# Summing q's squares with the squares as the stationary operand, one column of ones moving

## The reference, cut to what matters

```python
def _rmsnorm(x, w):
    var = jnp.mean(xf * xf, axis=-1, keepdims=True)      # over the 128 numbers of a head
    return (xf * jax.lax.rsqrt(var + EPS)).astype(x.dtype) * w
q = _rmsnorm(q, q_norm_w)
scores = jnp.einsum('bhqd,bhkd->bhqk', q, k) * scale
probs = jax.nn.softmax(scores.astype(jnp.float32), axis=-1)
```

## Time and profile before

| | us |
|---|---|
| median of three runs | 1466.25 |
| lowest, highest | 1464.45, 1468.65 |
| the profiled execution | 1465.77 |
| its span, first to last instruction | 1464.0 |
| TensorE busy | 1419.2 (97% of the span) |
| VectorE busy | 847.3 (58%) |
| ScalarE busy | 501.0 (34%) |
| GpSimd busy | 317.9 (22%) |

### The profile page before, as it was taken

How to read it: one execution, slowest core, us unless ns; L and a number is a source line. 1 busy time by engine, 2 the same in 40 slices (tenths; PEclk the granted TensorE clock), 3 DMA queues, 4 the chain that set the end, 5 groups by cost and what they waited for, 6 DMA issues and landing times.

```text
span 1464.0 us, 27092 instructions
## 1 busy us (share of the span) xinstructions
PE 1419.2 (97%) x9085; PEld 1128.1 (77%) x9086; DVE 847.3 (58%) x1816; ACT 501.0 (34%) x1097; POOL 317.9 (22%) x330
## 2 busy tenths in 40 slices
PE   6999997999999999999999999999999999999995
PEld 5888876787777877778787777877777888777773
DVE  5444446565666656666565666656687653344375
ACT  4333343333333333333333333333334421222220
POOL 1222223212122121211212121121212101232462
PEclk9999999999999999999999999999999999999997
DMA  6544440111111111111101111111122343655565
GB/s 225 164 122 136 122 118 30 47 30 40 37 40 40 30 47 37 34 36 40 41 29 49 37 33 39 38 40 33 59 71 81 126 170 138 230 164 170 153 195 171
DMA packets 91097, 125.95 MB, mean 86 GB/s; under 512 B 7376, under 2 KB 56528, under 8 KB 90512
## 3 DMA queue, kind: packets, MB, share of 16 engines
q1 hardware_dynamic: 84704, 104.16, 22.5%
q0 software_dynamic: 6320, 20.71, 5.1%
HBM read 87.36 MB, written 37.49 MB: 85 GB/s over the span
## 4 chain that ended last, share of the span: by engine, by line
PE 91%; issue 3%; DVE 2%; DMA 2%; POOL 1%; ACT 1%; SPq 0%; POOLq 0%; DVEq 0%; ACTq 0%
PE ps L549 23%; PE ps L551 22%; PE ps L550 22%; PE ps L879 5%; PE ps L615 4%; PE ps L657 4%; PE ps L895 3%; PE ps L623 2%; PE ps L642 2%; PE ps L874 1%; PE ps L596 1%; DMA acc<-in_wv 1%; DMA wgu<-in_w_gu 1%; DVE acc L1660 1%; PE ps L793 1%
## 5 line engine op out<-in xcount | busy, mean ns | idle before, releaser
L1046 ACT CAST ah<-ps 128x256 fp32r<-128x256 f32 x256 | 83.4, 382 | 238.5 <-PE ps L551 234.6
L470 POOL CAST vth<-vt 128x256 fp32r<-128x256 f32 x64 | 25.7, 402 | 637.6 <-PE ps L657 637.6
L1284 DVE TENSOR_TENSOR acc<-ps,acc 128x512 f32 (+1 forms) x129 | 88.6, 687 | 129.9 <-PE ps L551 129.9
L549 PE MATMUL ps<-hT,w0h 128*128 128x512 f32 (+1 forms) x384 | 153.9, 401 | 0.9 <-DVE w0l L1232 0.9
L551 PE MATMUL ps<-hT,w0h 128*128 128x512 f32 (+1 forms) x384 | 150.6, 392 | 0.0
L550 PE MATMUL ps<-hT,w0l 128*128 128x512 f32 (+1 forms) x384 | 150.0, 391 | 0.0
L464 POOL TENSOR_TENSOR qr<-qv,mhalf 128x8 f32<-128x8 f32 x64 | 105.6, 1649 | 90.0 <-DVE qv L1299 90.0
L1290 DVE TENSOR_TENSOR al<-ps,ah 128x256 fp32r<-128x256 f32 x256 | 95.7, 416 | 50.6 <-ACT ah L1046 50.6
L1013 ACT COPY qs<-ps 128x512 f32<-128x512 f32 x128 | 75.2, 587 | 134.9 <-PE ps L551 131.4
L1022 ACT ACTIVATE pb<-pb 128x256 f32<-128x256 f32 x128 | 48.2, 418 | 175.3 <-DVE pb L1315 175.3
L549 PE MATMUL ps<-w1l,ah 128*128 128x512 f32 x260 | 105.3, 405 | 1.0 <-DVE al L1290 1.0
(11 more groups left out here) (223 smaller groups left out, 3033.8 us busy)
## 6 DMA issues: line engine op xcount, KB each, us to landing
wraw<-in_w_att SPq DMA_DIRECT2D x64, 256.0 KB, 2.6
ybuf<-ye SPq DMA_DIRECT2D x47, 256.0 KB, 2.0
vbuf<-vo SPq DMA_DIRECT2D x16, 512.0 KB, 3.3
kbuf<-ko SPq DMA_DIRECT2D x16, 512.0 KB, 3.8
kt<-kbuf SPq DMA_DIRECT2D x32, 256.0 KB, 2.9
vt<-vbuf SPq DMA_DIRECT2D x64, 128.0 KB, 2.0
wgu<-in_w_gu SPq DMA_DIRECT2D x4, 2048.0 KB, 9.3
craw<-in_ctxT SPq DMA_DIRECT2D x9, 512.0 KB, 4.9
```

The source lines that it names most:

```text
L549: pe.matmul(dst, l_hi, r_lo, start=first, stop=False)
L1046: act.copy(ah[:, bp, :, b2, :], pv_view(bp, b2)).then_inc(a_hi, 1)
L1284: dve.tensor_tensor(dst, PS[6 + bp][:], dst, ALU.add).then_inc(acc_done, 1)
```

## The change

`q_sums` has its operands swapped. The squares of one head and one sequence, `sq[:, h, b]` (128 rows, 64 columns), are the weights, and one column of ones moves. A matmul gives 64 sums, one in each of 64 rows, in column `b` of bank 2; head 0 goes to rows 0 to 63 and head 1 to rows 64 to 127. Sixteen matmuls of one column stand in place of four of 256 columns. The sums then lie as the scores do, and VectorE reads the eight columns of bank 2 straight into `qv`. Its transpose, the tile `sst` and the semaphore `ss_turned` go; TensorE's two waits for `ss_turned` are for `q_var` now.

```diff
             def q_sums(j):
                 pe.wait_ge(q_sq, 2 * j + 2)
-                for r in range(4):
-                    s0 = 32 * (r % 2)
-                    mm = pe.matmul(PS[2][32 * r:32 * r + 32, 0:256], ones32[:], sq[:, r // 2, :, s0:s0 + 32],
-                                   start=True, stop=True)
+                for b in range(2 * CB):
+                    for h in range(2):
+                        mm = pe.matmul(PS[2][h * S:(h + 1) * S, b:b + 1], sq[:, h, b], ones32[:, 0:1],
+                                       start=True, stop=True)
                 mm.then_inc(ss_done, 1)
...
                 if last:
-                    pe.wait_ge(ss_turned, i + 1)
+                    pe.wait_ge(q_var, i + 1)
                     transpose_h2(0, 2)
...
                 if first:
                     pe.wait_ge(s_scaled, 1)
-                    pe.wait_ge(ss_turned, 1)
+                    pe.wait_ge(q_var, 1)
...
                 dve.wait_ge(ss_done, j + 2)
-
-                dve.transpose(sst[:].rearrange("p b r -> p (b r)"), PS[2][:, 0:256]).then_inc(ss_turned, 1)
-                dve.wait_ge(ss_turned, j + 1)
-                dve.tensor_scalar(qv[:], sst[:, :, 0], HD * EPS, None, ALU.add).then_inc(q_var, 1)
+                dve.tensor_scalar(qv[:], PS[2][:, 0:8], HD * EPS, None, ALU.add).then_inc(q_var, 1)
```

More of the change, by code:

```diff
@@ L152, in build @@
             pb = sb("pb", [P, 8, S], F32, a)
-            sst = sb("sst", [P, 8, 32], F32, a)
             pt = [sb(f"pt{'hl'[q]}", [P, 4, HG * S], F32R, a) for q in range(2)]
@@ L238, in build @@
             sem("s_sum"), sem("s_rcp"), sem("p_ready"))
-        ss_turned, v_split, pT_hi = sem("ss_turned"), sem("v_split"), sem("pT_hi")
+        v_split, pT_hi = sem("v_split"), sem("pT_hi")
         pT_done, pT_evac, pv_done, a_hi, a_lo, o_done, acc_done = (
```

## The result

| | before | after |
|---|---|---|
| median of 4 runs, us | 1467.21 | 1489.9 |
| lowest, highest | 1464.45, 1468.65 | 1488.27, 1491.15 |
| profiled execution | 1465.77 | 1490.86 |
| its span | 1464.0 | 1489.1 |

The account below looks back on a forecast made before the run. TensorE was taken to bound the kernel, with VectorE's time free from the third step on. 62 steps growing 0.32 us, less 0.3 at the start, add 19.5 us to 1465.77: 1485 us, range 1475 to 1496.

Parts of the forecast that it names:

- The bound: Whole kernel: TensorE, busy 97%, sets the time; removing VectorE's transpose, 0.47 us a step, is worth nothing in 62 steps.
- The terms at the two ends: First two steps: 0.3 us shorter in all; the last steps were counted among the 62 that grow.
- The pace of a pair, 0.058 us: Sums on TensorE: loading 64 fp32 weight columns holds each pair of passes at 0.058 us, as in the scores.
- The rival by which the pace goes with what moves: Sums: with one moving column a pair takes 25 ns, each step wins 0.21 us, kernel 1452 us; chance 0.06.
- passes in line: Sums: 32 passes of 25 ns one after another, growth 0.19 us a step, kernel 1477 us; chance 0.08.
- the prediction's upper bound: Sums: 16 pairs at 0.065 us, L841's pace, plus the whole 0.15 us switch; growth 0.48 us a step.
- The term of a step: Scores' last pass to the output projection: 1.03 us instead of 0.71, so each step grows by 0.32 us.
- the switch to the projection: Between the sums' last pass and the output projection's full array: 0.10 us.
- the forecast of 1.03 us for the new block: Scores' last pass to the projection: 0.93 us to the sums' last pass plus 0.10 for the switch.
- a forecast of 19.5 for steps and ends: Whole kernel: 62 steps growing by 0.32 us, 19.8 us, less 0.3 at the start.
- No change (a gap takes it up): Projection's first load, which stood 0.41 us with nothing named, would absorb up to that growth; kernel 1466 us; chance 0.04.
- The clock: Each step: longer low streaming drops the granted clock, six projection matmuls lose 1.3 us more, kernel 1566 us; chance 0.03.

Follow-up runs that it names:

- experiment 8: Kernel before with VectorE's transpose done twice in each softmax, one after the other; 1469.23 us, ratio 1.0022, middle steps still 14.18 us.
- experiment 4: Changed kernel with 32 columns of ones moving in each sums matmul instead of one; step 14.48 us, kernel 1493.45 us.
- experiment 5: Changed kernel with both heads' squares adjacent, 8 fp32 sums matmuls with 128 columns of weights instead of 16 with 64; step 15.37 us, kernel 1557.82 us.
- 6: Changed kernel with sums in 32 matmuls of 32 weight columns, in four quarters of the array; step 14.23 us, kernel 1466.77 us in one run.
- experiment 9: Swapped sums with 128 columns of weights, 8 matmuls, squares and ones in bf16 instead of fp32; 1437.76 us, ratio 0.9797 to the kernel before.
- The kernel without gaps: Changed kernel with 64 unused semaphore increments ahead of TensorE's program, moving its code by 4 KB; 1481.91 us, ratio 1.0102 to the kernel before.
- Experiment 3: Changed kernel with 240 unused semaphore increments ahead of TensorE's first instruction, outer loop's target at place 190 instead of 206; 1510.59 us, increments themselves 38.7 us.
- experiment 2: Kernel before with 80 unused semaphore increments ahead of TensorE's first instruction, outer loop's target at place 206 as in the changed kernel; 1473.87 us, ratio 1.0045.

## Why the prediction was right

**The bound.** That VectorE's transpose is worth nothing in the middle holds: 28.7 us less of VectorE, and the steps are longer (also experiment 8, with the sign turned). The terms at the two ends were off. The prediction let the first two steps become 0.3 us shorter in all; they became 0.33 longer (10.04 and 16.02 us against 10.25 and 15.48). TensorE's two waits in them are 1.9 us shorter together (2.31 and 3.20 against 2.85 and 4.53), but the granted clock from 229 to 250 us is 0.84 instead of 0.92, so TensorE's own work in that stretch takes longer. In the last steps 0.8 us came back: two of the three waits of the earlier trace rows stand there (0.70 at 1094.39 and 1.43 at 1111.56), and the first of them is gone. The prediction had counted those steps among the 62 in which nothing is won.

**The pace of a pair, 0.058 us, and its reason.** From the scores' second pair on it is 0.058, and in the sums it is the same. Experiments 4 to 6 show that the weights' columns set it, for ordinary fp32 matmuls. The rival by which the pace goes with what moves falls with experiment 4; that each pass or instruction has a price of its own (passes in line, 1477) falls with 5 and 6, where half as many instructions take twice as long and twice as many half as long. The rule of the Trainium skill that a matmul of one column takes as long as one of 60 ("TensorEngine Tiling (Array Packing)", Instruction Overhead) fits that 32 columns cost no more than one, but its 25 ns does not give this kernel's time; only the bf16 passes of experiment 9 start every 25 ns. What does is the load's rule ("TensorE: Matmul & The Clock Gate", LDWEIGHTS), columns divided by 1.2: 53 ns for 64, 27 for 32, 107 for 128, each 4 to 5 ns under the pace measured.

One row was misread. L841, the prediction's upper bound and its argument against the rival of what moves, is a transpose: 48 columns move, but its weights have 128 (48*128 in the earlier trace rows), in one pass each. It is not of the scores' form, so it neither bounded the pair nor spoke against that rival. And at 65 ns for 128 fp32 columns it is faster than the 112 ns of experiment 5, so what was found for matmuls does not hold for transposes.

**The term of a step.** 0.32 was said and 0.287 measured, 2.0 us too much over 62 steps. From the scores' last pass to the projection the growth is 0.31 by the starts in the trace. Two parts of it were off, in opposite ways: the sums' second pair follows the first after 0.03 us instead of 0.058, and the switch to the projection was priced at 0.10 and is 0.127. So the forecast of 1.03 us for the new block was met to 0.002 by errors that cancel. Then the projection's first twelve matmuls take 0.025 us less than before, and no run shows why.

**What was missing.** The profiled execution before, the steps' growth and what came back at both ends give 1465.8 + 18.1 - 0.25 - 0.8 = 1482.8. The kernel without gaps took 1481.9 and the kernel after 1489.9. By the steps' lengths 6.6 of the 22.7 us come from the two jumps and from one stretch of half clock behind them, which no term of the prediction has. So that 1485 was near is partly luck: a missing 6.6 us and a forecast of 19.5 for steps and ends, where 17.0 was measured, point opposite ways.

The cause was in the code: 48 more instructions in each of 7 copies of the sums ahead of the outer loop move its target by 336 places. The Trainium skill has the rule ("Runtime: NRT & Kernel Launch", Instruction fetch mechanics): instructions come in blocks of 16 KB, ahead of time only in sequence, and a jump to code outside the window has to wait for its block. The trace agrees: packets of 16 KB, and a wait of 3.3 to 3.4 us at both jumps, in the kernel before as well as after. TensorE itself need not stand still for it. The first wait is covered by what its queue holds; the second, for the block behind the target's, is covered if enough instructions of the target's own block are left, and in the kernel after only three were. By experiment 3 each matmul more in that block takes 0.17 to 0.20 us off the gap.

**No change (a gap takes it up)** fell: the whole growth stands between the scores and the projection (1.64 to 1.97 us). The 0.41 us was idle time of the loads alone, and the sums' own loads fill it now. **The clock** did not fall in the middle steps of the kernel after, except behind the second gap; it did so at the start, as said, and in ten steps of experiment 5.

## What to carry to other kernels

An fp32 matmul with few moving columns costs what its weights' load costs, so before operands are swapped to spare another engine a transpose, count the passes (those in different parts of the array once) and multiply by the load of their weight columns; here a pair of passes with 64 fp32 columns took 58 ns. Work taken from an engine that is not waited for gave nothing back: 28.7 us less of VectorE, and the middle steps grew. When an edit changes how many instructions lie ahead of a long loop, look behind the loop's jump for idle time with nothing named, and compare with code moved by a few KB before the edit is blamed or praised.

## What had not been expected of the hardware

- A jump target three instructions ahead of the end of a 16 KB block: 2.0 and 2.4 us of idle TensorE at the two jumps, and 6.6 us of 1490 with the half clock behind the second. The jump's own wait of 3.3 to 3.4 us is there in every kernel and cost TensorE nothing.
- fp32 passes in two halves or four quarters of the array go on beside each other: 58 ns for a pair of 64 columns of weights, 31 for four of 32, where one of 128 takes 112.
- The granted clock over the first two steps differs between profiles with the same softmax (0.92 in the kernel before, 0.76 in experiment 2) and these steps are 1.6 us longer with the lower one. In experiment 5 it fell to 1.2 GHz in ten steps, behind 2.9 us of scores and sums with short matmuls.
